# Routing weights applied to the experts' inner values, eight experts summed in one PSUM bank

## The chip, the cores and the metric

The kernel is one program on one core of a Trainium2 chip. A core has five engines with instruction streams of their own, which meet only at semaphores: TensorE (PE, matrix products into PSUM), VectorE (DVE), ScalarE (ACT), GpSimd (POOL) and SyncE (SP, which here issues all DMAs). The metric is the device time of one execution in microseconds (us).

## The reference, cut to what matters

The program is two layers of attention and feed-forward with a layer norm ahead of and behind each. The change lies in the last part, a mixture of eight experts over 2 x 1024 tokens of width 128:

```python
weights = _routing_weights(x, Wr, temperature)      # [tokens, 8]
gate = jnp.einsum('btd,edi->beti', x, Wg)           # inner size I = 128
up = jnp.einsum('btd,edi->beti', x, Wu)
h = jax.nn.silu(gate) * up
e_out = jnp.einsum('beti,eid->betd', h, Wd)
out = jnp.einsum('bte,betd->btd', weights, e_out)
...
x = x + _layernorm(out)                             # of x = _layernorm(...) going in
```

The routing weights come from a sigmoid of `x @ Wr`, a window on its value, two exponentials, and a fallback on the two best experts.

## The kernel before, in words

Tokens are handled in four chunks of 512; two chunks make one batch. In the expert stage the 32 pairs of chunk `c` and expert `e` are numbered n = 8c + e. All data are float32. Every order is written out by hand, in one loop for each engine, and an engine that waits in its list holds up all that stands behind it.

For each n TensorE computes gate and up (`d_up`, L573: two products of 128x512) into one of two pairs of PSUM banks, ScalarE takes silu of the gate (L791), VectorE multiplies by up (`d_hidden`, L1207) into one of two buffers `h_d`, and TensorE multiplies by the expert's down weights (`d_down`, L582: four products of 128x128), one expert behind, so ups and downs alternate. Tokens stand on the partitions of the result, so the routing weight of expert e is one number per partition and block: VectorE multiplies the bank with it (`d_scale`, L1217), and GpSimd adds the eight results of a chunk into `y_a` (L1452 for the first, L1455 for the rest). Then come a layer norm and the addition to `x`: statistics on VectorE (`stats`, L830 and L833), the inverse root on GpSimd (`rstd_of`, L1295 and L1296), the application (`apply`, L840, four parts) and the addition (L850) on VectorE.

Other work is threaded into these loops. The routing weights of the first batch (`route_a`, `route_b`, `route_c`, L1098 to L1138) are computed on VectorE ahead of the loops, those of the second batch within them. The second half of the preceding attention is finished here as well: its head norms (`heads_square`, `heads_b`), the turning of its result (`d_turn_y`), the output product (`d_wo`), its norm c_out of chunks 2 and 3, and the norm d_in, the turning (`d_turn_x`) and the router products of these chunks, without which the experts of chunks 2 and 3 can't begin. GpSimd's inverse roots are done in the order of the table `NORMS`; `apply` waits for the count of its entry.

## Time and profile before

| what | value |
|---|---|
| device time, median of 3 runs | 828.21 us (826.44 to 828.77) |
| span of the profiled execution, first to last instruction | 824.3 us |
| TensorE / VectorE / ScalarE / GpSimd busy in the span | 703.1 / 596.4 / 486.6 / 259.7 us |
| last add of the stage ends (L850) | 821.6 us after the span's start |
| first up product of the stage starts (L573) | 688.1 us |
| mean granted TensorE clock | 0.974 of full speed |

The page gives the profiled execution's time as its span; the runs' median is 3.9 us more, which lies around the span. Times on the trace are counted from the span's start. The expert stage is the last 136 us. Busy time of TensorE counts overlapping, modelled ends, so its share in a stretch says how seldom it waited, not how fast it ran.

### The profile page before, as it was taken

How to read it: one execution, taken by the hardware profiler on the slowest of the kernel's cores; microseconds unless marked ns; L12 is line 12 of the kernel's file. 1: busy time of each engine (PE TensorE's matmuls, PEld its weight loads, DVE VectorE, ACT ScalarE, POOL GpSimd, SP SyncE). 2: the span in 40 equal slices, each digit the busy share in tenths (PEclk: the TensorE clock that was granted, in tenths of full speed). 3: DMA queues.
4: the chain of work that ended last, by engine and by line, in shares of the span. 5: the costliest groups of instructions: out<-in, count | busy, mean ns of one | idle time of the engine just before them, and what ended most of it. 6: DMA issues, size and time to landing. Idle time of an engine off the chain costs nothing.

```text
span 824.3 us, 9749 instructions
## 1 busy us (share of the span) xinstructions
PE 703.1 (85%) x3471; PEld 297.3 (36%) x3512; DVE 596.4 (72%) x1107; ACT 486.6 (59%) x467; POOL 259.7 (32%) x373
## 2 busy tenths in 40 slices
PE   5999899999997689888888988888888884797695
PEld 2576445454544122222222222222222221465353
DVE  4656413226163988988998899999999987669765
ACT  1344424243432688998999999899888883121221
POOL 3601000001026461334226334423330004355254
PEclk9999999999999799999999999999999998799898
DMA  8000200000000000000000000000000000000000
GB/s 285 0 2 2 79 0 0 1 1 0 0 1 0 1 1 1 0 2 1 1 1 1 1 1 0 1 1 1 1 1 1 0 1 1 0 1 14 0 14 26
DMA packets 7152, 9.15 MB, mean 11 GB/s; under 512 B 1216, under 2 KB 5952, under 8 KB 6720
## 3 DMA queue, kind: packets, MB, share of 16 engines
q1 hardware_dynamic: 7104, 8.53, 3.0%
q8 instruction: 28, 0.46, 0.2%
q14 instruction: 20, 0.16, 0.1%
HBM read 7.48 MB, written 1.05 MB: 10 GB/s over the span
## 4 chain that ended last, share of the span: by engine, by line
PE 48%; DVE 35%; ACT 9%; issue 6%; POOL 1%; DMA 1%; SPq 0%; POOLq 0%; DVEq 0%; ACTq 0%
DVE hid L1018 10%; DVE hid L1015 10%; PE ps L453 7%; PE ps L463 7%; ACT probs L740 6%; PE ps L524 6%; PE ps L531 6%; PE ps L573 4%; PE ps L440 3%; PE ps L313 2%; PE ps L582 2%; PE ps L473 2%; PE ps L360 2%; PE ps L391 2%; DVE st L830 1%
## 5 line engine op out<-in xcount | busy, mean ns | idle before, releaser
L756 ACT ACTIVATE w_hh<-hid 128x2048 f32<-128x2048 f32 x128 | 243.8, 1904 | 10.3 <-DVE hid L1018 9.9
L524 PE MATMUL ps<-q_s,k 128*128 128x512 bf16 x496 | 147.5, 387 | 54.4 <-DVE hid L1018 38.2
L1015 DVE TENSOR_TENSOR hid<-ps,probs 128x1024 f32<-128x1024 f32 x128 | 156.2, 1221 | 34.1 <-ACT probs L740 32.7
L740 ACT ACTIVATE probs<-ps,gain 128x1024 f32<-128x1024 f32 x128 | 142.2, 1111 | 46.0 <-PE ps L524 45.4
L1018 DVE SCALAR_TENSOR_TENSOR hid<-ps,probs 128x1024 f32<-128x1024 f32 x128 | 155.5, 1215 | 0.0
L531 PE MATMUL ps<-w_hh,v_h 128*32 128x512 f32 x1024 | 138.1, 611 | 2.1 <-ACT w_hh L756 1.6
L524 PEld LDWEIGHTS ps<-q_s,k 128*128 128x128 bf16 x512 | 37.5, 98 | 150.9 <-DVE hid L1018 90.2
L524 PE MATMUL ps<-q_s,k_s 128*128 128x512 bf16 x231 | 72.3, 386 | 3.4 <-DVE q_s L1029 1.3
L926 DVE SCALAR_TENSOR_TENSOR hid<-ps,s_b,rot 128x512 f32<-128x512 f32 x16 | 11.9, 750 | 87.1 <-ACT rot L713 87.1
L791 ACT ACTIVATE hid<-ps 128x512 f32<-128x512 f32 x32 | 19.0, 598 | 89.0 <-PE ps L573 86.9
L1295 POOL TENSOR_SCALAR rs<-mv 128x4 f32<-128x4 f32 x32 | 7.3, 229 | 172.1 <-DVE mv L833 171.6
L582 PE MATMUL ps<-probs_t,hid 128*128 128x128 f32 x256 | 37.7, 294 | 27.4 <-DVE hid L1207 20.7
L453 PE MATMUL ps<-hid,w_hh 128*128 128x512 f32 x128 | 56.0, 595 | 0.0
L463 PE MATMUL ps<-hid,w_hh 128*128 128x512 f32 x128 | 55.6, 592 | 0.0
L1333 POOL TENSOR_SCALAR u_k<-part 128x128 bf16<-128x128 bf16 x96 | 48.3, 530 | 9.7 <-DVE part L982 9.7
L582 PEld LDWEIGHTS ps<-probs_t,hid 128*128 128x128 f32 x256 | 34.9, 204 | 44.8 <-DVE hid L1207 29.4
L1333 POOL TENSOR_SCALAR u_q<-part 128x128 bf16<-128x128 bf16 x96 | 48.4, 532 | 0.0
L1455 POOL TENSOR_TENSOR y_a<-y_a,hid 128x512 f32<-128x512 f32 x28 | 35.9, 1282 | 25.5 <-DVE hid L1217 24.5
L531 PEld LDWEIGHTS ps<-w_hh,v_h 128*32 128x32 f32 x1024 | 20.6, 108 | 57.8 <-issue 55.2
L524 PEld LDWEIGHTS ps<-q_s,k_s 128*128 128x128 bf16 x256 | 18.2, 98 | 61.0 <-issue 33.6
L1207 DVE TENSOR_TENSOR hid<-ps,hid 128x512 f32<-128x512 f32 x32 | 21.8, 685 | 24.2 <-ACT hid L791 24.0
L1352 POOL TENSOR_SCALAR v_h<-v_c 128x128 f32<-128x128 f32 x16 | 8.9, 554 | 92.4 <-PE ps L531 92.4
(220 smaller groups left out, 958.7 us busy)
## 6 DMA issues: line engine op xcount, KB each, us to landing
w_hh<-in_b_h SPq DMA_DIRECT2D x2, 1024.0 KB, 8.1
x_res<-in_x SPq DMA_DIRECT2D x4, 256.0 KB, 6.4
tab<-in_rope SPq DMA_DIRECT2D x1, 1024.0 KB, 7.7
out<-x_res SPq DMA_DIRECT2D x4, 256.0 KB, 2.3
w<-in_b_w SPq DMA_DIRECT2D x1, 512.0 KB, 5.6
tab<-in_d_wg SPq DMA_DIRECT2D x1, 512.0 KB, 3.5
tab<-in_d_wu SPq DMA_DIRECT2D x1, 512.0 KB, 4.4
probs_t<-in_d_wd SPq DMA_DIRECT2D x1, 512.0 KB, 4.9
```

The source lines that it names most:

```text
L453: last = mm(ps[:, o, :], w_h1[:, k, o * P:(o + 1) * P], hid[:, 0, k, :], start=(k == 0), stop=(k == KT_ - 1))
L463: last = mm(ps[:, o, :], w_h2[:, k, o * P:(o + 1) * P], hid[:, 1, k, :], start=(k == 0), stop=(k == KT_ - 1))
L524: last = mm(ps[:, base + half, :], k_op[:, u, keys], q_s[:, u, half * CHUNK:(half + 1) * CHUNK], start=True, stop=True)
L531: last = mm(ps[VW * g4:VW * g4 + VW, 6, :], v_h[:, u, mt, :], ee[:, mt % 2, g4 * CHUNK:(g4 + 1) * CHUNK], start=(mt == 0), stop=(mt == BT ...
L573: last = mm(ps[:, 2 * (e % 2) + w, :], wt[:, e, :], xt_d[c], start=True, stop=True)
L582: last = mm(ps[:, 4 + e % 2, k * P:(k + 1) * P], h_d[:, e % 2, k * P:(k + 1) * P], w_d[:, e, :], start=True, stop=True)
L740: A(gg[:, mt % 2, :], banks[:, 0:2 * CHUNK], ACT.Tanh, scale=gain[:, u:u + 1]).then_inc(S["g"], 1)
L756: A(ee[:, mt % 2, :], zz[:, mt % 2, :], ACT.Exp).then_inc(S["e"], 1)
L1015: v.tensor_tensor(zz[:, mt % 2, 0:SEQ], banks[:, 2 * CHUNK:4 * CHUNK], gg[:, mt % 2, :], ALU.add).then_inc(S["z1"], 1)
L1018: v.scalar_tensor_tensor(zz[:, mt % 2, SEQ:2 * SEQ], banks[:, 4 * CHUNK:6 * CHUNK], -1.0, gg[:, mt % 2, :], ALU.mult, ALU.subtract).then_i ...
L1333: last = g.tensor_scalar(out_ap, in_ap, 1.0, None, ALU.mult)
L1455: g.tensor_tensor(y_d(c), y_d(c), e_out[:, e % 2], ALU.add).then_inc(S["ad_d"], 1)
```

## The change

The routing weight is applied before the down product instead of after it. There the token runs along the free dimension, so the weight has to be a row of 512 numbers that is the same on all 128 partitions. Once the weights of a batch are computed (`wts`), TensorE turns them (`d_turn_w`), ScalarE copies the 64x128 result to `w_t`, SyncE writes it to a DRAM tensor `w_rows`, waits until it has landed, and reads it back in four transfers, each with four experts' rows of 512 repeated for 128 partitions (1 MB each in SBUF). GpSimd multiplies `h_d` by them in place (32 times), and the down products of a chunk's eight experts add up in one PSUM bank. The multiplication by the weight on VectorE (L1217, 32 times) and the 32 copies and additions on GpSimd (L1452, L1455) are gone; the statistics and the application of the last norm read PSUM.

`h_d` becomes a ring of 12 slots. In each batch the first eleven ups run with no down between them; behind ups 11 to 14 stand three downs each and behind the last one four. The routing of the first batch is laid between the first `d_hidden` calls, that of the second batch behind those of n = 21, 23 and 24, and the attention's rest stands at other n. `NORMS` has a new order: c_out 2, c_out 3, d_in 2, d_in 3, d_out 0.

```diff
-         ("d_in", 1), ("c_out", 2), ("d_out", 0), ("d_in", 2), ("c_out", 3), ("d_in", 3), ("d_out", 1),
+         ("d_in", 1), ("c_out", 2), ("c_out", 3), ("d_in", 2), ("d_in", 3), ("d_out", 0), ("d_out", 1),
...
+ND = CHUNKS * EXPERTS
+SLOTS = 12
+
+
+def downs_after(n):
+
+    b, i = divmod(n, ND // BATCH)
+    if i == ND // BATCH - 1:
+        return n + 1
+    return b * (ND // BATCH) + (min(3 * (i - SLOTS + 2), i - 1) if i >= SLOTS - 1 else 0)
...
-        wts = sb("wts", [P, BATCH, BT, EXPERTS])
-        sg_d, h_d = (flat_hid[:, 2 * CHUNK * i:2 * CHUNK * (i + 1)].rearrange("p (a b) -> p a b", a=2)
-                     for i in range(2))
-        e_out = flat_hid[:, 4 * CHUNK:6 * CHUNK].rearrange("p (a b c) -> p a b c", a=2, b=CT)
+        wts = sb("wts", [P, BATCH, EXPERTS, BT])
+        w_t = sb("w_t", [P // 2, P])
+        w_rows = nc.dram_tensor("w_rows", (BATCH, EXPERTS, SEQ), F32, kind="Internal").ap()
+        sg_d = u_q[:].rearrange("p a b c -> p (a b c)").bitcast(F32).rearrange("p (a b) -> p a b", a=2)
+        h_d = flat_hid.rearrange("p (a b) -> p a b", a=SLOTS)
+        flat_hh = w_hh[:].rearrange("p a b c -> p (a b c)")
+        part_f = [w[:].rearrange("p a b c -> p (a b c)").bitcast(F32) for w in part[:2]]
+        half_e = EXPERTS // 2
+        w_b = [[flat_hh[:, i * half_e * CHUNK:(i + 1) * half_e * CHUNK].rearrange("p (a b) -> p a b", a=half_e)
+                for i in range(2)], [w.rearrange("p (a b) -> p a b", a=half_e) for w in part_f]]
...
+            for b in range(BATCH):
+                sp.wait_ge(S["wt_d"], b + 1)
+                sp.dma_start(w_rows[b].rearrange("e (t k) -> (e t) k", t=BT), w_t[:]).then_inc(S["w_out"], 16)
+                sp.wait_ge(S["w_out"], 16 * (b + 1))
+                for half in range(2):
+                    if b:
+                        sp.wait_ge(S["hw_d"], EXPERTS * (half + 1))
+                    for g in range(2):
+                        src = w_rows[b][g * half_e:(g + 1) * half_e, half * CHUNK:(half + 1) * CHUNK]
+                        sp.dma_start(w_b[half][g], src.unsqueeze(0).to_broadcast([P, half_e, CHUNK])
+                                     ).then_inc(S[f"w_in{half}{g}"], 16)
...
             def d_down(c, e):
                 n = EXPERTS * c + e
-                pe.wait_ge(S["h_d"], n + 1)
-                if n >= 2:
-                    pe.wait_ge(S["sc_d"], n - 1)
+                pe.wait_ge(S["hw_d"], n + 1)
+                if c >= 2 and e == 0:
+                    pe.wait_ge(S["xfin"], c - 1)
                 for k in range(CT):
-                    last = mm(ps[:, 4 + e % 2, k * P:(k + 1) * P], h_d[:, e % 2, k * P:(k + 1) * P],
-                              w_d[:, e, :], start=True, stop=True)
+                    last = mm(ps[:, 4 + c % 2, k * P:(k + 1) * P], h_d[:, n % SLOTS, k * P:(k + 1) * P],
+                              w_d[:, e, :], start=(e == 0 and k == 0), stop=(e == EXPERTS - 1),
+                              skip_group_check=True)
                 last.then_inc(S["eo_d"], 1)
...
+            def d_turn_w(b):
+                pe.wait_ge(S["wts_d"], b + 1)
+                if b:
+                    pe.wait_ge(S["xt_d"], 2)
+                nc.tensor.transpose(ps[0:P // 2, BANK_TURN, 0:P], wts[:, b].rearrange("p e t -> p (e t)"),
+                                    ident[:]).then_inc(S["wtp_d"], 1)
...
-            for c in range(CHUNKS):
-                for e in range(EXPERTS):
-                    d_up(c, e)
...
+            downs = 0
+            for n in range(ND):
+                c, e = divmod(n, EXPERTS)
+                d_up(c, e)
+                if n in (8, 25):
+                    d_turn_w(n // 16)
+                if n in (10, 11):
+                    d_turn_y(n - 8)
+                if n in (11, 12):
+                    d_wo(n - 9)
+                for m in range(downs, downs_after(n)):
+                    d_down(*divmod(m, EXPERTS))
+                downs = max(downs, downs_after(n))
+                if n in (14, 16):
+                    d_turn_x(n // 2 - 5)
+                if n == 18:
+                    d_route(2)
                     d_route(3)
...
+            def d_wt(b):
+                act.wait_ge(S["wtp_d"], b + 1)
+                if b:
+                    act.wait_ge(S["w_out"], 16)
+                A(w_t[:], ps[0:P // 2, BANK_TURN, 0:P], ACT.Copy).then_inc(S["wt_d"], 1)
+
             d_gate(0)
             d_exps(0)
-            for c in range(CHUNKS):
-                for e in range(EXPERTS):
-                    n = EXPERTS * c + e
...
+            for n in range(ND):
+                e = n % EXPERTS
+                act.wait_ge(S["gu_d"], n + 1)
+                if n >= 2:
+                    act.wait_ge(S["h_d"], n - 1)
+                A(sg_d[:, e % 2, :], ps[:, 2 * (e % 2), :], ACT.Silu).then_inc(S["sg_d"], 1)
+                if n in (8, 25):
+                    d_wt(n // 16)
+                if n in (10, 11):
+                    d_yt(n - 8)
+                if n in (14, 16):
+                    d_xt(n // 2 - 5)
+                if n == 20:
                     d_gate(1)
+                if n == 22:
+                    d_exps(1)
...
-            def d_hidden(c, e):
-                n = EXPERTS * c + e
+            def d_hidden(n):
+                e = n % EXPERTS
                 dve.wait_ge(S["sg_d"], n + 1)
-                if n >= 2:
-                    dve.wait_ge(S["eo_d"], n - 1)
-                v.tensor_tensor(h_d[:, e % 2, :], ps[:, 2 * (e % 2) + 1, :], sg_d[:, e % 2, :],
+                if n >= SLOTS:
+                    dve.wait_ge(S["eo_d"], n - SLOTS + 1)
+                v.tensor_tensor(h_d[:, n % SLOTS, :], ps[:, 2 * (e % 2) + 1, :], sg_d[:, e % 2, :],
                                 ALU.mult).then_inc(S["h_d"], 1)

-            def d_scale(c, e):
-
-                n = EXPERTS * c + e
...
+            def sum_d(c):
+                return ps[:, 4 + c % 2, :].rearrange("p (a b) -> p a b", a=CT)
...
+            def d_out_add(c):
+                apply("d_out", c, sum_d(c), y_d(c))
+                v.tensor_tensor(x_of(c), x_of(c), y_d(c), ALU.add).then_inc(S["xfin"], 1)
...
             route_a(0)
-            route_b(0)
-            route_c(0)
-            for c in range(CHUNKS):
...
+            for n in range(ND):
+                d_hidden(n)
+                if n == 0:
+                    route_b(0)
+                if n == 2:
+                    route_c(0)
+                if n == 6:
+                    heads_square(1)
+                    for i in range(3):
+                        rsqrt_newton(rstd[:, 0:W2], W2, "ms_o" if i == 2 else None)
+                if n == 11:
+                    wo_bias(2)
+                    stats("c_out", 2, y[:])
+                if n == 12:
+                    add_out("c_out", 2, y[:])
+                    wo_bias(3)
+                    stats("c_out", 3, y[:])
+                    stats("d_in", 2, x_of(2))
+                if n == 13:
+                    d_in_apply(2)
+                    add_out("c_out", 3, y[:])
+                    stats("d_in", 3, x_of(3))
+                if n == 14:
+                    d_in_apply(3)
+                if n in (15, 17, 30):
+                    d_out_stats({15: 0, 17: 1, 30: 2}[n])
+                if n in (16, 18, 31):
+                    d_out_add({16: 0, 18: 1, 31: 2}[n])
+                if n == 19:
                     dve.wait_ge(S["rt_d"], 2)
                     for half in range(2):
                         logits(half, ps[:, 6, half * CT * EXPERTS:(half + 1) * CT * EXPERTS]).then_inc(S["z_d"], 1)
+                if n == 21:
+                    route_a(1)
+                if n == 23:
+                    route_b(1)
+                if n == 24:
+                    route_c(1)
             d_out_stats(CHUNKS - 1)
-            add_out("d_out", CHUNKS - 1, y_d(CHUNKS - 1), "xfin")
+            d_out_add(CHUNKS - 1)
...
-            for c in range(CHUNKS):
-                for e in range(EXPERTS):
-                    n = EXPERTS * c + e
...
+            heads_b(1)
+            for n in range(ND):
+                c, e = divmod(n, EXPERTS)
+                b, half = divmod(c, 2)
+                pool.wait_ge(S["h_d"], n + 1)
+                if e % half_e == 0:
+                    pool.wait_ge(S[f"w_in{half}{e // half_e}"], 16 * (b + 1))
+                g.tensor_tensor(h_d[:, n % SLOTS, :], h_d[:, n % SLOTS, :], w_b[half][e // half_e][:, e % half_e, :],
+                                ALU.mult).then_inc(S["hw_d"], 1)
+                if n in (2, 3):
+                    rstd_of("c_out", n)
+                if n in (5, 7):
+                    rstd_of("d_in", n // 2)
+                if n in (13, 15, 29):
+                    rstd_of("d_out", {13: 0, 15: 1, 29: 2}[n])
             rstd_of("d_out", CHUNKS - 1)
```

TensorE around n = 6 to 9, before. L573 is an up product (two rows each), L582 a down product, L313 a turning, L597 the output product.

```order
L573 MATMUL ps<-xt,tab 128x512 x2
L582 MATMUL ps<-probs_t,hid 128x128 x4
L313 MATMUL ps<-ident,xn_c 128x128 x4
L573 MATMUL ps<-xt,tab 128x512 x2
L582 MATMUL ps<-probs_t,hid 128x128 x4
L597 MATMUL ps<-w_os,w 128x128 x4
L582 MATMUL ps<-probs_t,hid 128x128 x4
L573 MATMUL ps<-xt_c,tab 128x512 x2
```

TensorE from n = 9 to 13 now. L602 is the up product, L611 the down product, L342 and L620 turnings, L636 the output product.

```order
L602 MATMUL ps<-xt_c,tab 128x512 x4
L342 MATMUL ps<-ident,xn_c 128x128 x4
L602 MATMUL ps<-xt_c,tab 128x512 x2
L342 MATMUL ps<-ident,y_c 128x128 x4
L636 MATMUL ps<-w_os,w 128x128 x4
L611 MATMUL ps<-probs_t,hid 128x128 x12
L602 MATMUL ps<-xt_c,tab 128x512 x2
L636 MATMUL ps<-w_os,w 128x128 x4
L611 MATMUL ps<-probs_t,hid 128x128 x12
L602 MATMUL ps<-xt_c,tab 128x512 x2
L611 MATMUL ps<-probs_t,hid 128x128 x12
```

Before, one down follows each up; now the first three downs (12 products of L611) stand behind the twelfth up and both turnings, and the thirteenth up stands behind these three.

GpSimd, chunks 0 and 1, before: L1452 and L1455 are the sums, L1295 with L1296 an inverse root.

```order
L1455 TENSOR_TENSOR y_a<-y_a,hid 128x512 x5
L1295 TENSOR_SCALAR rs<-mv 128x4
L1296 TENSOR_TENSOR rs<-rs,half_down 128x4
L1452 TENSOR_SCALAR y_a<-hid 128x512
L1295 TENSOR_SCALAR rs<-mv 128x4
L1296 TENSOR_TENSOR rs<-rs,half_down 128x4
L1455 TENSOR_TENSOR y_a<-y_a,hid 128x512
```

GpSimd now: L1490 is the multiplication by the routing weights, L1333 with L1334 an inverse root.

```order
L1490 TENSOR_TENSOR hid<-hid,w_hh 128x512 x3
L1333 TENSOR_SCALAR rs<-mv 128x4
L1334 TENSOR_TENSOR rs<-rs,half_down 128x4
L1490 TENSOR_TENSOR hid<-hid,w_hh 128x512
L1333 TENSOR_SCALAR rs<-mv 128x4
L1334 TENSOR_TENSOR rs<-rs,half_down 128x4
L1490 TENSOR_TENSOR hid<-hid,w_hh 128x512 x2
```

The inverse roots now stand between multiplications for which the down products wait: c_out 2 behind n = 2, c_out 3 behind n = 3, d_in 2 behind n = 5 (and, not shown, d_in 3 behind n = 7, d_out 0 behind n = 13, d_out 1 behind n = 15).

## Rows read from the trace of the kernel before

**Rows 1.** Busy us by stretch and engine (instructions), clock, DMA share, GB/s.
```profile
777.00:814.00 37.00, 35.36 (x154) 22.23 (x155) 24.90 (x46) 7.19 (x12) 20.82 (x18) 0.94 0.05 15
```

**Rows 2.** Chain that ended last, expert stage: start, us, engine, tile, line, count.
```profile
807.93 1.72 PE ps L573 x4
809.65 0.89 PE ps L582 x8
...
729.62 0.44 PE ps L313 x4
...
817.00 0.88 DVE st L830 x4
817.91 0.39 DVE mv L833 x4
...
820.90 0.69 DVE x_res L850
```

**Rows 3.** Waits of TensorE, 704 to 825: total, times, longest.
```profile
PE ps L582 <- DVE hid L1207: 20.7, 7, 13.1
PE ps L582 <- DVE hid L1217: 6.4, 1, 6.4
```

**Rows 4.** Timeline of TensorE: start, us, instruction, idle before it and releaser.
```profile
704.92 2.07 PE L582 MATMUL ps<-probs_t,hid 128*128 128x128 f32 x8 [13.10 <-DVE hid L1207]
...
706.79 3.20 PE L573 MATMUL ps<-xt,tab 128*128 128x512 f32 x4
...
719.30 1.16 PE L582 MATMUL ps<-probs_t,hid 128*128 128x128 f32 x8 [1.48 <-DVE hid L1207]
...
743.79 2.07 PE L582 MATMUL ps<-probs_t,hid 128*128 128x128 f32 x8 [3.29 <-DVE hid L1207]
```

**Rows 5.** Timeline of VectorE and ScalarE: routing, head norms, table load.
```profile
693.05 1.08 DVE L1109 TENSOR_TENSOR w_a<-w_a 128x64 f32<-128x64 f32 x1
...
700.27 0.69 DVE L1117 TENSOR_REDUCE w_a<-raw 128x64 f32<-128x512 f32 x1
...
703.92 0.22 DVE L1138 TENSOR_TENSOR wts<-w_a,rs 128x64 f32<-128x64 f32 x1
...
714.47 0.68 DVE L1084 TENSOR_REDUCE ms_o<-probs_t 128x32 f32<-128x512 f32 x1
...
718.41 0.23 DVE L818 SCALAR_TENSOR_TENSOR rstd<-nt,rstd 128x64 f32<-128x64 f32 x1
...
763.68 1.28 ACT L770 ACT_TABLE_LOAD   x1
```

**Rows 6.** Groups by line, 687.5 to 825: count, busy us, mean ns, idle before.
```profile
L1455 POOL TENSOR_TENSOR y_a<-y_a,hid 128x512 f32<-128x512 f32 x28 | 35.9, 1282 | 25.5 <-DVE hid L1217 24.5
...
L1207 DVE TENSOR_TENSOR hid<-ps,hid 128x512 f32<-128x512 f32 x32 | 21.8, 685 | 24.2 <-ACT hid L791 24.0
...
L791 ACT ACTIVATE hid<-ps 128x512 f32<-128x512 f32 x32 | 19.0, 598 | 89.0 <-PE ps L573 86.9 <-DVE hid L1207 2.0
...
L1296 POOL TENSOR_TENSOR rs<-rs,half_down 128x4 f32<-128x4 f32 x8 | 8.4, 1052 | 0.7
```

**Rows 7.** Timeline of VectorE: the four-part apply (L840), three cases.
```profile
752.64 2.06 DVE L840 TENSOR_SCALAR y_a<-y_a,mv,rs 128x128 f32<-128x128 f32 x4
...
780.35 3.01 DVE L840 TENSOR_SCALAR y_a<-y_a,mv,rs 128x128 f32<-128x128 f32 x4
...
819.75 1.11 DVE L840 TENSOR_SCALAR y_a<-y_a,mv,rs 128x128 f32<-128x128 f32 x4 [1.47 <-POOL rs L1296]
```

**Rows 8.** DMA issues: tile, queue, count, KB each, us to landing.
```profile
w_hh<-in_b_h SPq DMA_DIRECT2D x2, 1024.0 KB, 8.1
...
out<-x_res SPq DMA_DIRECT2D x4, 256.0 KB, 2.3
...
w<-in_b_w SPq DMA_DIRECT2D x1, 256.0 KB, 9.7
```

**Rows 9.** Busy time by stretch, while three weight loads run.
```profile
92.00:94.00 2.00, 2.00 (x6) 0.89 (x5) 0.00 (x0) 0.96 (x1) 0.27 (x1) 1.00 1.04 420
```

More of the change, by code:

```diff
@@ L229, in sandwich @@
             ro to_a ms_o yc ytp yt wo wo_read xn_d tp_d xt_d rt_d z_d tanh_d dist_d ex_d
-            gu_d sg_d h_d eo_d sc_d ad_d xfin stored""".split()
+            gu_d sg_d h_d hw_d eo_d wts_d wtp_d wt_d w_out w_in00 w_in01 w_in10 w_in11 xfin stored""".split()
         S = {n: sem("e_" + n) for n in names}
@@ L604, in d_turn_x @@
                     pe.wait_ge(S["xt_d"], c - 2)
-                turn_chunk(xn).then_inc(S["tp_d"], 1)
+                turn_chunk(xn_2[c % 2]).then_inc(S["tp_d"], 1)
             def d_route(c):
@@ L1119, in route_c @@
             def route_c(b):
-                w = wts[:, b]
+                w = wts[:, b].rearrange("p e t -> p t e")
                 wide = [P, BT, EXPERTS]
@@ L1137, in route_c @@
                 me.step(v.reciprocal(rs1[:, 2], rs1[:, 0]))
-                me.step(v.tensor_tensor(w, rt[:, 3], rs1[:, 2].unsqueeze(2).to_broadcast(wide), ALU.mult))
+                v.tensor_tensor(w, rt[:, 3], rs1[:, 2].unsqueeze(2).to_broadcast(wide), ALU.mult).then_inc(S["wts_d"], 1)
             turn_out(("k", 0))
@@ new lines, in d_out_stats, with d_in_apply @@
+                dve.wait_ge(S["eo_d"], EXPERTS * (c + 1))
+                stats("d_out", c, sum_d(c))
+            def d_out_add(c):
+                apply("d_out", c, sum_d(c), y_d(c))
+                v.tensor_tensor(x_of(c), x_of(c), y_d(c), ALU.add).then_inc(S["xfin"], 1)
+            def d_in_apply(c):
+                if c == 3:
+                    dve.wait_ge(S["ytp"], 1)
+                else:
+                    dve.wait_ge(S["turned"], turns_done(("x", 1)))
+                apply("d_in", c, x_of(c), xn_2[c % 2][:], "xn_d")
@@ L1442, in _ @@
             heads_a(1)
-            for c in range(CHUNKS):
-                for e in range(EXPERTS):
-                    n = EXPERTS * c + e
-                    pool.wait_ge(S["sc_d"], n + 1)
-                    if e == 0:
-                        if c >= 2:
-                            pool.wait_ge(S["xfin"], c - 1)
-                        g.tensor_scalar(y_d(c), e_out[:, 0], 1.0, None, ALU.mult).then_inc(S["ad_d"], 1)
-                    else:
-                        pool.wait_ge(S["ad_d"], n)
-                        g.tensor_tensor(y_d(c), y_d(c), e_out[:, e % 2], ALU.add).then_inc(S["ad_d"], 1)
-                    at = (c, e)
-                    if at == (0, 2):
-                        heads_b(1)
-                    if at == (0, 7):
-                        rstd_of("c_out", 2)
-                    if at == (1, 0):
-                        rstd_of("d_out", 0)
-                    if at == (1, 1):
-                        rstd_of("d_in", 2)
-                        rstd_of("c_out", 3)
-                    if at == (1, 3):
-                        rstd_of("d_in", 3)
-                    if c >= 2 and e == 0:
-                        rstd_of("d_out", c - 1)
+            heads_b(1)
[13 more added lines that the diff above has]
+                    rstd_of("d_out", {13: 0, 15: 1, 29: 2}[n])
             rstd_of("d_out", CHUNKS - 1)
```

78 lines of the change are left out of this document (3 added, 75 removed).

## The prediction

> **What bounds the kernel now.** I read the stretches first. Late in the expert stage (777 to 814 us) TensorE is busy 35.4 of 37 us [rows 1], but over the whole stage it isn't. The chain of waits gives what it needs there: an up product 1.72 us, a down product 0.89, a turning 0.44 [rows 2]. The stage has 32 ups (55.0), 32 downs (28.5), four turnings (1.8), and two output and two router products of eight passes each like a down (3.6): 88.8 us. From the first up at 688.1 to the end of the last down at about 814.5 are 126.4 us. The difference of 37.6 us has two parts. TensorE waited for VectorE's products and scalings 20.7 + 6.4 us, 13.1 of it once, while VectorE computed the first routing weights [rows 3], and 1.4 us elsewhere. The other 9 us are a lower clock: behind waits of 13.1 and 3.3 us a down took 2.07 us instead of 1.16, behind 1.5 us it did not [rows 4]. So the stage is bound by lists of four engines that wait for each other, and by TensorE's work in its second half. VectorE's 0.69 us scaling and GpSimd's 1.28 us sum per expert [rows 6] mostly lie beside TensorE. Behind the last down come 7.1 us to the last addition.
>
> **How I work it out.** I laid the new lists of all engines end to end: each instruction starts when its engine is free and what it waits for has ended, with durations of the rows. The old lists laid out so end at 821.2 us; the trace has 821.6. I add that 0.4.
>
> Durations: up 1.72, down 0.89 [rows 2]; silu 0.60, `d_hidden` 0.64 to 0.69 [rows 6]; statistics 1.25 and the addition 0.69 [rows 2]; an inverse root 1.4 from the end of the statistics to the apply (817.91 + 0.39 to 819.75) [rows 2, 7]. GpSimd's multiplication is not in the trace; the nearest row is its sum of two SBUF operands of the same 512 at 1.28 us, and I take that. Its bounds are 1.05 (the cheapest GpSimd row, L1296) and 1.4 (two VectorE products of 0.69 one behind the other) [rows 6].
>
> The apply has three prices: 1.11 us with GpSimd idle, 2.06 and 3.01 with its sums under way [rows 7]. By my layout GpSimd waits during most applies of the new lists, so they get 1.11, but d_in 3 gets 3.0 and d_out 2 gets 2.06. The Trainium skill, "SBUF — State Buffer", section "Who interferes with whom", says that VectorE's two-port modes and its instructions with two SBUF inputs share one port pair with GpSimd, a lock held for the whole instruction. By that rule 1.11 would hold wherever GpSimd waits, as the rows say; if instead 2.06 held for five of these applies, the sum would be 4.3 us higher.
>
> DMA: `w_rows` is written in 2.3 us, as the 256 KB stores are [rows 8]. While three weight loads run, the queues move 420 GB/s [rows 9], which is 2.5 us for 1 MB. The first of the four broadcasts lands 2.3 + 2.5 = 4.8 us after its issue, the others 2.5 us apart. The trace has no transfer that reads one place 128 times. Bounds: 2.3 us for the first load, if its bytes cost nothing beyond a small transfer, and upward 8.1 us for each 1 MB one behind the other (the landing of `w_hh`), or even 38.8 us, if a megabyte moved at the worst row, 256 KB in 9.7 us [rows 8]. I take the rate of rows 9, since size and partitions are those of its loads.
>
> **The change part by part, by TensorE's waits.**
> - Start. `d_hidden(0)` stands behind `route_a` and the scalar engine's exponentials, `d_hidden(1)` and (2) behind `route_b`, which takes 7.2 us beside GpSimd's `heads_a`. Up 2 waits 3.2 us (to 694.8), up 3 4.4 us (to 702.6). The routing weights, ready at 704.1 before [rows 5], are ready at 706.4 but no longer hold TensorE 13.1 us. The head norms (714.47 to 718.64, 4.2 us [rows 5]) behind n = 6 hold up 9 for 2.5 us.
> - First weights. `d_turn_w(0)` stands behind up 8 and ends at 715.1; copy 0.3, store 2.3 and first load 4.8 lead to 723.0. Up 11, both turnings and output product 2 cover this: down 0 starts at 724.6 and the three downs wait 0.6 together.
> - n = 12. The root of c_out 3 stands on GpSimd ahead of multiplication 4. It needs statistics that VectorE makes behind `d_hidden(12)`, apply, addition, bias. Up 12 ends 729.5; 0.6 + 0.7, then 1.1 + 0.7 + 0.7 + 1.2 give 734.6; root 1.3 and multiplication 1.3 give 737.2. TensorE ended down 3 at 731.3: a wait of 5.9.
> - n = 13. Up 13 ends 742.7, its product 744.0; apply d_in 2, apply and addition c_out 3 and statistics d_in 3 (1.1 + 1.1 + 0.7 + 1.2) lead to 748.2, root and multiplication 8 to 750.8. TensorE ended down 7 at 744.5: a wait of 6.4.
> - n = 15. Root d_out 0 stands ahead of multiplication 14 and needs statistics behind `d_hidden(15)`, 762.8: multiplication 14 ends 765.4, TensorE waits 3.4. Down 15 ends at 769.0.
> - Ups 16 to 25 run at 1.72 each, with two waits of 0.8 together at most, then the second routing: `d_hidden(23)` waits for two table loads (1.28 each [rows 5]) and the exponentials, `route_b` takes 3.5 (five wide operations of 0.69 [rows 5]), `route_c` 3.1. Up 25 waits 1.6, the turning of weights, placed behind it, waits 5.5 more, until 795.7.
> - Second weights. Copy, store, load and first multiplication take 8.8 us behind 796.2; only ups 26 and 27 cover it. Down 16 waits 3.7 and starts at 805.0.
> - From there 16 downs and four ups are 21.1 us, a restart 1.9: the last down ends at 828.1. GpSimd, 16 multiplications and a root, keeps just ahead.
> - Behind it: 4.9 us (statistics 1.2, 0.5 late since d_out 2 is just being added, root 1.4, apply 1.1, addition 0.7) instead of 7.1, since scaling and sum are gone.
>
> The clock: seven waits above are over 3 us (3.2, 4.4, 5.9, 6.4, 3.4, 5.5, 3.7). The rows give 0.9 us for the down alone behind 3.3 us, and 2.07 + 3.20 against 1.16 + 1.72, or 2.4, behind 13.1 [rows 2, 4]. I take 1.9 each, 13.4 in all, against 9.1 now.
>
> The sum for TensorE: work 89.3, waits 37.3, clock 13.4 = 140.0 us, from 688.1 to 828.1. Against now: work +0.5, waits +8.8 (37.3 against 28.5), clock +4.3, tail -2.2: 11.4, with rounding 11.5. The span would be 835.8 us instead of 824.3. The runs lie 3.9 us above the span, so 828.2 + 11.6 = 839.8, **840 us**, 1.4% slower. What is removed, 22 us of VectorE and 42 of GpSimd, was hidden except in the tail; GpSimd gets 41 us of multiplications back.
>
> **The rivals.**
> 1. The broadcast loads are slow. For: all 128 partitions read the same 8 KB, which no row shows. Against: every row of large transfers is near 400 GB/s. At 8.1 us each, the last group of weights lands 20 us later in either batch (32.4 against 12.3); laid out, the span is 850.4, the time 854. At 38.8 us each it is 1080 (time 1084). The Trainium skill, "SBUF — State Buffer", section "A bandwidth-pool intuition that's wrong (but worth ruling out)", gives 22.5 GB/s for one port of the HBM crossbar; if all reads fell on one, 1 MB would take 47 us by that page, an estimate, beyond even my worst row.
> 2. Waits of 3 to 6 us leave the clock up. For: behind 1.5 us it stayed. Against: 3.3 us was enough once. All seven restarts off give a span of 828.4, time 832; with a multiplication of 1.04 and the fastest loads besides, 824.2, time 828: no change.
> 3. Faster: GpSimd's roots don't hold the multiplications, because VectorE reaches the statistics of c_out 3, d_in 3 and d_out 0 early, so that downs 4, 8 and 14 find their operand. That takes off 15.7 us of waits and three restarts of 1.9: 840 - 21.4 = 818 us. It decides from where these three waits fall below 2.5 us in all. Against: up 12 and up 13 stand behind the downs that wait, so VectorE can't be early; this is in the lists, not in durations.
>
> **How the numbers follow.** The forecast, 833 to 847, has 0.62. Rival 1 has 0.20, rival 2 0.12 (half of it at 826 to 831), rival 3 0.06. A measurement tells 0.3%, 2.5 us, from no change. Faster by more: 0.06. Within: 0.06, all from rival 2. Slower: 0.88. The range leaves out rival 3 and the far part of rival 1: 829 to 862.
>
> **What would show it.** TensorE should wait once each at the down products 4, 8 and 14 for GpSimd, about 6, 6 and 3 us, and for VectorE at the second turning of weights, 5 to 6. The four broadcasts should land 4.8 us after issue and 2.5 apart, the multiplication should take 1.3, the clock should fall behind each wait over 3 us, and the last down should end 4 to 5 us ahead of the last addition. I am wrong if the multiplications take clearly over 1.3 (with 1.6 the span is 840.4), if a broadcast takes over 6 us, or if TensorE doesn't wait at downs 4 and 8.

## The result, and the profile after

The changed kernel takes 843.29 us (median of 4 runs, 840.16 to 843.8), the kernel before beside it 827.43 (826.44 to 828.77): a ratio of 1.0184, 95% interval 1.0168 to 1.0200. It is slower, by 1.8%. The forecast was 840, within 829 to 862. The profiled execution has a span of 838.4 us, where 835.8 was worked out.

By stretch, in the columns of [rows 1]:

```profile
688.00:704.00 16.00, 8.82 (x15) 3.30 (x16) 14.64 (x29) 3.37 (x6) 9.51 (x8) 0.73 0.00 1
704.00:736.00 32.00, 24.25 (x95) 13.49 (x94) 18.54 (x62) 7.22 (x13) 9.88 (x11) 0.93 0.41 132
736.00:777.00 41.00, 30.13 (x135) 22.19 (x136) 11.97 (x42) 4.58 (x8) 18.18 (x18) 0.79 0.00 1
777.00:814.00 37.00, 25.90 (x81) 13.72 (x81) 16.77 (x50) 9.16 (x17) 9.36 (x9) 0.91 0.33 110
```

From 777 to 814 TensorE was busy 35.4 us before [rows 1] and is busy 25.9 now: the stretch that TensorE filled has become one of waits. Between 736 and 777 the mean clock is 0.79. No other engine is near full there (VectorE 12 of 41 us, GpSimd 18): nothing is overloaded, the lists wait for each other. The waits of TensorE, 686 to 840, against [rows 3]:

```profile
PE ps L611 <- POOL hid L1490: 19.9, 4, 6.4
PE ps L602 <- DVE hid L1254: 11.6, 5, 4.2
PE ps L620 <- DVE wts L1185: 5.4, 1, 5.4
```

The timeline of TensorE at these waits (L602 up, L611 down, L620 turning of weights; L1490 is GpSimd's multiplication, L1254 the inner value), against [rows 4]:

```profile
694.63 3.05 PE L602 MATMUL ps<-xt,tab 128*128 128x512 f32 x4 [2.98 <-DVE hid L1254]
701.88 10.71 PE L602 MATMUL ps<-xt,tab 128*128 128x512 f32 x20 [4.20 <-DVE hid L1254]
...
736.98 3.78 PE L611 MATMUL ps<-probs_t,hid 128*128 128x128 f32 x16 [6.09 <-POOL hid L1490]
740.55 3.20 PE L602 MATMUL ps<-xt_c,tab 128*128 128x512 f32 x4
743.58 1.95 PE L611 MATMUL ps<-probs_t,hid 128*128 128x128 f32 x16
751.92 2.08 PE L611 MATMUL ps<-probs_t,hid 128*128 128x128 f32 x8 [6.39 <-POOL hid L1490]
...
767.32 3.56 PE L611 MATMUL ps<-probs_t,hid 128*128 128x128 f32 x16 [3.50 <-POOL hid L1490]
...
798.06 0.42 PE L620 MATMUL ps<-ident,wts 128*64 128x128 f32 x1 [5.35 <-DVE wts L1185]
...
807.21 4.70 PE L611 MATMUL ps<-probs_t,hid 128*128 128x128 f32 x24 [3.87 <-POOL hid L1490]
```

Behind the wait of 6.09 us two downs take 3.57 us from start to start and the up 3.03, against 1.78 and 1.72 at full clock. From 743.58 on two downs show 1.95, so the clock is back. On GpSimd the waits of 6.09, 6.39 and 3.50 us end in the same way (the first two are shown; the one of 3.87 ends with a DMA landing):

```profile
734.34 0.23 POOL L1333 TENSOR_SCALAR rs<-mv 128x4 f32<-128x4 f32 x1 [5.47 <-DVE mv L880]
734.66 1.03 POOL L1334 TENSOR_TENSOR rs<-rs,half_down 128x4 f32<-128x4 f32 x1
735.66 2.49 POOL L1490 TENSOR_TENSOR hid<-hid,w_hh 128x512 f32<-128x512 f32 x2
...
749.29 0.23 POOL L1333 TENSOR_SCALAR rs<-mv 128x4 f32<-128x4 f32 x1 [7.37 <-DVE mv L880]
749.61 1.03 POOL L1334 TENSOR_TENSOR rs<-rs,half_down 128x4 f32<-128x4 f32 x1
750.61 7.39 POOL L1490 TENSOR_TENSOR hid<-hid,part 128x512 f32<-128x512 f32 x6
```

GpSimd idles 5.5 and 7.4 us for statistics (`mv`), makes the inverse root, and only then multiplies the value that TensorE wants; six multiplications had piled up behind the second. The DMA issues, in the columns of [rows 8]:

```profile
w_hh<-w_rows SPq DMA_DIRECT2D x4, 1024.0 KB, 7.4
part<-w_rows SPq DMA_DIRECT2D x4, 1024.0 KB, 12.7
```

These are medians of four, two in each batch. All four loads of a batch are issued together, so later ones count the time of those ahead. The first lands within 5.5 us of its issue at 716.92 (GpSimd's first multiplication starts at 722.43), the slowest load 13.7 us after its own issue. The transfers of the first batch end at about 731.6.

### The profile page after: what moved, and what is told of

Same layout as the page of the kernel before. It is cut to its first block, busy times and chain, and to the rows that moved or that the text cites. A ratio compares the mean times of both kernels' runs of the same rounds, so it can differ in the third digit from the quotient of the medians.

```text
span 838.4 us, 9688 instructions
## 1 busy us (share of the span) xinstructions
PE 716.5 (85%) x3514; PEld 302.1 (36%) x3514; DVE 569.4 (68%) x1075; ACT 486.7 (58%) x469; POOL 256.9 (31%) x373
## 3 DMA queue, kind: packets, MB, share of 16 engines
HBM read 15.87 MB, written 1.11 MB: 20 GB/s over the span
## 4 chain that ended last, share of the span: by engine, by line
PE 49%; DVE 32%; ACT 9%; issue 5%; DMA 2%; POOL 2%; SPq 0%; POOLq 0%; ACTq 0%; DVEq 0%
DVE hid L1065 10%; DVE hid L1062 10%; PE ps L482 7%; PE ps L492 7%; PE ps L553 6%; ACT probs L780 6%; PE ps L560 6%; PE ps L602 4%; PE ps L611 3%; PE ps L469 3%; PE ps L342 2%; PE ps L502 2%; PE ps L389 2%; PE ps L420 2%; DMA w_hh<-w_rows 1%
## 5 line engine op out<-in xcount | busy, mean ns | idle before, releaser
L553 PE MATMUL ps<-q_s,k 128*128 128x512 bf16 x512 | 151.0, 387 | 51.4 <-DVE hid L1065 36.0
L553 PE MATMUL ps<-q_s,k_s 128*128 128x512 bf16 x256 | 77.8, 386 | 1.1 <-DVE q_s L1076 1.1
L836 ACT ACTIVATE u_q<-ps 128x512 f32<-128x512 f32 x32 | 18.9, 597 | 101.1 <-PE ps L602 101.0
L1254 DVE TENSOR_TENSOR hid<-ps,u_q 128x512 f32<-128x512 f32 x32 | 21.9, 689 | 71.3 <-ACT u_q L836 71.1
L1333 POOL TENSOR_SCALAR rs<-mv 128x4 f32<-128x4 f32 x32 | 7.3, 229 | 193.7 <-DVE mv L880 193.3
L611 PE MATMUL ps<-probs_t,hid 128*128 128x128 f32 x256 | 37.7, 309 | 20.0 <-POOL hid L1490 19.9
L611 PEld LDWEIGHTS ps<-probs_t,hid 128*128 128x128 f32 x256 | 36.1, 221 | 26.1 <-POOL hid L1490 22.0
L1387 POOL TENSOR_SCALAR gain<-gains 128x1 f32<-128x1 f32 x16 | 3.8, 236 | 104.7 <-ACT probs L780 104.7
```

The source lines that it names most:

```text
L553: last = mm(ps[:, base + half, :], k_op[:, u, keys], q_s[:, u, half * CHUNK:(half + 1) * CHUNK], start=True, stop=True)
L611: last = mm(ps[:, 4 + c % 2, k * P:(k + 1) * P], h_d[:, n % SLOTS, k * P:(k + 1) * P], w_d[:, e, :], start=(e == 0 and k == 0), stop=(e == ...
```

## The experiments

Each ran three rounds beside the kernel before; times are medians, spans those of the profiled executions. All but the run on the kernel before are edits of the changed kernel.

**Roots later in GpSimd's list.**

```diff
-                if n in (2, 3):
-                    rstd_of("c_out", n)
-                if n in (5, 7):
-                    rstd_of("d_in", n // 2)
...
+                if n in (2, 7):
+                    rstd_of("c_out", {2: 2, 7: 3}[n])
+                if n in (7, 11):
+                    rstd_of("d_in", {7: 2, 11: 3}[n])
+                if n == 15:
+                    rstd_of("d_out", 0)
+                    rstd_of("d_out", 1)
```

> The changed kernel with five of GpSimd's inverse roots moved back behind multiplications that don't need them: c_out 3 and d_in 2 behind n = 7 (were 3 and 5), d_in 3 behind n = 11 (was 7), d_out 0 behind n = 15 (was 13). No instruction is added or removed. Theory A (the order of GpSimd's list holds down products 4, 8 and 14 by 6.1, 6.4 and 3.5 us, and each such wait brings 1.6 to 3.1 us of lower clock): laying the lists out gives a wait of 2 us at down 8 and none at 4 and 14, a span near 817 instead of 838.4, so about 822 us, 2.5% under the changed kernel and below the kernel before (827.4). Rival B (VectorE's work at n = 12 and 13 is what ends last; the roots only mark it): the waits move to the applies and stay, span above 833, time above 836.

Measured 827.95 us (10 runs), ratio to before 1.0007, 0.9989 to 1.0024; span 826.6. The waits at downs 4 and 14 are gone (one of 1.1 us is left at down 15), and 15.3 of the 15.9 us that the change had cost came back: with the roots out of the way the loss is gone. But 822 was expected, from a span of 817. Of these 9.6 us of span 2.9 lie ahead of down 0, which starts at 726.84 here and at 723.99 in the changed kernel, although the lists are the same up to there. The lower clock was held longer in this execution; first the changed kernel's row, then this one's:

```profile
687.95 3.70 PE L602 MATMUL ps<-xt,tab 128*128 128x512 f32 x8 [0.53 <-DVE qkv_a L1078]
```

```profile
688.59 6.41 PE L602 MATMUL ps<-xt,tab 128*128 128x512 f32 x8 [0.53 <-DVE qkv_a L1078]
```

The larger part lies behind it. VectorE's applies, and GpSimd's row of multiplications beside each:

```profile
732.68 4.04 DVE L887 TENSOR_SCALAR y<-y,mv,rs 128x128 f32<-128x128 f32 x4
...
742.36 4.89 DVE L887 TENSOR_SCALAR xn<-x_res,mv,rs 128x128 f32<-128x128 f32 x4 [1.12 <-POOL rs L1334]
747.17 1.10 DVE L887 TENSOR_SCALAR y<-y,mv,rs 128x128 f32<-128x128 f32 x4
```

```profile
730.46 6.18 POOL L1490 TENSOR_TENSOR hid<-hid,w_hh 128x512 f32<-128x512 f32 x5
...
742.22 4.94 POOL L1490 TENSOR_TENSOR hid<-hid,part 128x512 f32<-128x512 f32 x4
```

A set of four parts takes 4.04 and 4.89 us while GpSimd multiplies, and 1.10 once it has stopped (747.17). A third took 3.92. That is some 9.5 us more on VectorE than at 1.1 each. The wait at down 8 was 4.6 us instead of the 2 expected. That the slow applies are the whole of the rest isn't shown: no run on these lists has them fast.

**Filler products in TensorE's waits.** Of products whose results aren't used, 6 stand before down 4, 6 before down 8, 3 before down 14, 5 before the second turning of weights and 3 before down 16.

```diff
+            def keep_busy(at, pe):
...
+                for i in range(count):
+                    mm(ps[:, bank, :], ident[:], xt_c[:], start=True, stop=True)
```

> The changed kernel with products that nobody reads put into TensorE's five long waits (6, 6, 3, 5 and 3 products of 128x512 float32 at 0.86 us, ahead of down products 4, 8, 14, of the second turning of weights and of down product 16). It leaves nothing out. Theory A (about 10 us of the changed kernel's time is TensorE at half the clock behind these waits: 3.1, 2.5, 1.6, 1.6, 1.9 by its trace): the products behind them run at 0.89 and 1.72, the span falls by 7 to 10 us to about 830, since some of it comes back as longer waits for the loads. Rival B (the clock behind a wait costs nothing, as GpSimd's 1.25 us per expert sets the pace there): the span stays within 2 us of 838.4, or grows by fillers that run past the end of a wait.

Measured 836.39 us, ratio 1.0105 (1.0084 to 1.0126), 6.9 below the changed kernel. The span is 835.4, only 3.0 below, where 7 to 10 were expected. But this execution, too, came late to the part that the filler touches: down 0 starts at 728.11 instead of 723.99. From there to the end of the last down it is 99.7 us against 106.8, 7.1 less. Behind the wait at down 4 two downs and the up now run at full clock:

```profile
740.55 2.38 PE L611 MATMUL ps<-probs_t,hid 128*128 128x128 f32 x16 [0.94 <-POOL hid L1501]
742.77 1.88 PE L602 MATMUL ps<-xt_c,tab 128*128 128x512 f32 x4
...
804.42 4.57 PE L611 MATMUL ps<-probs_t,hid 128*128 128x128 f32 x24 [2.73 <-POOL hid L1501]
```

Against 3.78 and 3.20 us above (the 2.38 contain a wait for multiplication 5). At down 16 the three products of filler were too few: a wait of 2.7 us was left, and the three downs behind it still take 4.42 us from start to start, against 4.54 above and 2.67 at full clock. So the clock was lost through the waits. Where about 1 us of wait was left, at four of the five places, it stayed up, and what came back is the lower end of what theory A named.

**One set of weights.** The second batch takes the first batch's weights: its turning, store and loads are left out.

```diff
-            for b in range(BATCH):
+            for b in range(1):
...
-                if n in (8, 25):
-                    d_turn_w(n // 16)
+                if n == 8:
+                    d_turn_w(0)
```

> The changed kernel without the second trip of the weights: no second turning, copy, store or loads, and GpSimd multiplies the second batch by the first batch's weights (so the output of the second batch is weighted wrongly; VectorE still computes its weights). Theory A (the second trip costs TensorE 5.4 us ahead of the turning and 3.9 ahead of down product 16, and two restarts of the clock, less what VectorE's routing then holds): the span falls by 9 to 10 us to about 829. Rival B (VectorE's routing at n = 23 and 24 holds TensorE just as long at the ups behind it): under 5 us. Rival C (GpSimd's 16 multiplications from n = 16 on bound the end): they start earlier too, so it agrees with A; it would be seen by waits at each down product.

Measured 836.89 us, ratio 1.0121 (1.0102 to 1.0141): 6.4 less, between the two expectations. The waits of 5.4 and 3.9 us are gone, but VectorE's routing then holds an up, which was covered before:

```profile
796.42 3.78 PE L602 MATMUL ps<-qkv_a,tab 128*128 128x512 f32 x4 [3.32 <-DVE hid L1254]
```

TensorE's waits for VectorE's inner values rose from 11.6 to 16.8 us: more than half of the 9.2 us removed came back, by the way that rival B named. The span fell by 4.0 us, the median by 6.4.

**The kernel before, with its first two inner values ahead of the routing.**

```diff
             route_a(0)
+            d_hidden(0, 0)
             route_b(0)
+            d_hidden(0, 1)
             route_c(0)
```

> The kernel before with one part of the change alone, routing in pieces: the products of n = 0 and 1 on VectorE stand behind route_a and route_b instead of behind all three. Theory A: TensorE's wait of 13.1 us becomes waits of about 3, 3 and 2 us, downs 0 and 1 are done before the weights are ready; laid out, the span falls by 5.8 us to 818.5, time about 821.6. Rival B (the scalings need the weights anyway, and TensorE waits at down 2 for what it saved): the span within 2 us of 824.3.

Measured 821.48 us, ratio 0.9933 (0.9919 to 0.9948), as expected to 0.2 us; the span is 819.9, for 818.5. The one wait of 13.1 us in [rows 3] has become two, of 1.6 and 4.2 us (about 3, 3 and 2 were expected). From 686 us on:

```profile
PE ps L582 <- DVE hid L1207: 12.9, 8, 4.2
```

So the routing in pieces is worth 6 us by itself, and the changed kernel, which has it too, lies 22 us above this one.

**Applies with three operands** (those of c_out and d_in for chunks 2 and 3), on the roots-later kernel, and as a control on the changed kernel.

```diff
                 for k in range(CT):
+                    if kind in ("c_out", "d_in") and c >= 2:
+                        last = v.scalar_tensor_tensor(dst[:, k, :], src[:, k, :], mv[:, i, k, 0:1],
+                                                      rs[:, i, k:k + 1].to_broadcast([P, P]), ALU.subtract, ALU.mult)
+                        continue
                     last = v.tensor_scalar(dst[:, k, :], src[:, k, :], mv[:, i, k, 0:1], rs[:, i, k:k + 1],
                                            ALU.subtract, ALU.mult)
```

> The kernel with the roots later (the run before), with one thing more: the c_out and d_in applies of chunks 2 and 3 are written as scalar_tensor_tensor, (x - mean) * rstd with rstd broadcast along the row as the third operand, in place of tensor_scalar. Same reads, same writes, same place in VectorE's list, one operand more. Theory A: the tensor_scalar from SBUF is held until GpSimd's row of multiplications has ended (4.04, 4.89 and 3.92 us in the run before, each ending within 0.4 us of the end of GpSimd's row), and the form with three operands isn't: then each set of four takes 1.3 to 1.5 us, the waits for the two chunks' experts shrink, and the time falls by 7 to 11 us, to 817 to 821 us. Rival B: any VectorE work with SBUF operands slows beside GpSimd's multiplications (both move the same bytes): then the four take 3 us or more and the time stays at 826 to 830.

> Control: the changed kernel with only the form of these applies changed as in the run beside it; the roots stay where the change has them. GpSimd is idle while these applies run (1.11 us for four, all four sets), so both theories expect nothing to win: four would take 1.3 to 1.4 us in place of 1.11, and the time stays within 1.5 us of the changed kernel's 843.3 (842 to 845). Should it come out 3 us or more faster, the gain of the run beside it would not be the port's but the form's.

Measured 828.08 us (10 runs, ratio 1.0016, 0.9998 to 1.0035) and 843.02 (1.0207, 1.0176 to 1.0237). The control came as expected; the first did not: the sets took 4.26, 5.10 and 4.09 us.

```profile
732.20 0.69 DVE L1258 TENSOR_TENSOR hid<-ps,u_q 128x512 f32<-128x512 f32 x1 [3.02 <-ACT u_q L836]
...
742.69 5.10 DVE L888 SCALAR_TENSOR_TENSOR xn<-x_res,mv,rs 128x128 f32<-128x128 f32 x4 [1.11 <-POOL rs L1338]
747.71 1.13 DVE L888 SCALAR_TENSOR_TENSOR y<-y,mv,rs 128x128 f32<-128x128 f32 x4
```

My choice of form was poor: it reads two tensors from SBUF. The Trainium skill, "SBUF — State Buffer", section "Who interferes with whom", has that case beside the two-port modes as the two that take the ports shared with GpSimd, and these runs agree: part by part, one beside the row takes 1.30 us in the old form and 1.35 in the new, about one multiplication of 1.25, against 0.33 and 0.34 alone. (In the sets of 4.04 and 3.92 us one part of the four ran free.) Rival B got the time right, and is wrong only in its "any": an inner value (one operand in PSUM, one in SBUF) takes 0.69 us beside the row too (732.20), and an apply from PSUM isn't slowed. In the changed kernel the last but one apply has a multiplication beside it:

```profile
828.10 1.36 DVE L887 TENSOR_SCALAR y_a<-ps,mv,rs 128x128 f32<-128x128 f32 x4
828.26 1.27 POOL L1490 TENSOR_TENSOR hid<-hid,part 128x512 f32<-128x512 f32 x1 [0.59 <-DVE hid L1254]
...
833.55 1.37 DVE L887 TENSOR_SCALAR y_a<-ps,mv,rs 128x128 f32<-128x128 f32 x4 [1.47 <-POOL rs L1334]
```

1.36 us beside GpSimd, 1.37 without. The next two kernels have lists laid out before this was known, on theory A's 1.4 us for every apply.

**All lists rewritten**, with either form of the apply.

```diff
+PE_TURN_W = {6: 0, 22: 1}
+PE_TURN_X = {14: 2, 16: 3}
+ROOTS = {1: ['c2'], 5: ['c3', 'di2'], 9: ['di3'], 14: ['do0'], 17: ['do1'], 29: ['do2']}
+DVE_STEPS = {1: ['rb0a', 'rb0b'], 2: ['rb0c', 'rb0d'], 4: ['rc0a', 'rc0b'], 5: ['hsqa'], ...}
...
+                for name in DVE_STEPS.get(n, ()):
+                    step[name]()
```

> The changed kernel (broadcast weights, one bank per sum, ring of 12) with the order of every list written anew: first routing cut into six pieces between the hidden values of experts 1 to 4, first weights turned behind up 6 (not 8), the second routing's steps behind hidden values 16 to 20 and its weights turned behind up 22 (not 25), no root in GpSimd's list ahead of a multiplication that a down waits for (roots behind multiplications 1, 5, 9, 14, 17, 29), downs spread between the ups from up 10 on, applies with three operands. Laid end to end with the measured durations (up 1.72, down 0.89, multiplication 1.25, apply 1.4) TensorE waits 3.1 us at up 2 and under 1 us anywhere else, the last down ends near 786, and the span is 793: time 794 to 802. Theory A (the loss of the change is its waits, their clock, and a list that leaves VectorE no room): within that. Rival B (the broadcast's DMAs and 32 multiplications on GpSimd slow the others once they run side by side): 808 or more.

> The same lists as the run beside it, with the applies in the old form (tensor_scalar). Under theory A (port held by GpSimd's rows) at least two of the four sets of applies fall beside a row of multiplications and take 3 to 5 us: 3 to 10 us more than the run beside it, 800 to 808. Under B of the first of these runs: within 1.5 us of the run beside it.

Measured 810.53 us (ratio 0.9803, 0.9780 to 0.9825) and 810.33 (0.9801, 0.9785 to 0.9817): faster than every kernel so far, 8.5 to 16.5 us above theory A's 794 to 802, in rival B's range (808 or more), and no difference between the forms. In the first of the two:

```profile
720.56 5.18 DVE L896 SCALAR_TENSOR_TENSOR y<-y,mv,rs 128x128 f32<-128x128 f32 x4 [0.89 <-POOL rs L1346]
...
732.41 5.12 DVE L896 SCALAR_TENSOR_TENSOR xn<-x_res,mv,rs 128x128 f32<-128x128 f32 x4 [0.96 <-POOL rs L1346]
...
742.75 5.10 DVE L896 SCALAR_TENSOR_TENSOR xn_c<-x_res,mv,rs 128x128 f32<-128x128 f32 x4 [1.53 <-POOL rs L1346]
```

Each of these follows on a root, and so does GpSimd's row of multiplications: a root ends, both engines start, and they collide all three times. Three sets at 5.1 instead of 1.4 are 11 us on VectorE, and TensorE waited 2.5, 2.1 and 2.8 us behind them. So rival B was right that the multiplications slow VectorE once they run side by side; of the broadcasts' DMAs this doesn't show it.

**The apply in two instructions over 512 elements**: on the roots-later kernel, on these lists, and on lists laid out again with 2.7 us for an apply.

```diff
+                if kind in ("c_out", "d_in") and c >= 2:
+                    me.step(v.tensor_tensor(dst, src, mv[:, i, :, 0:1].to_broadcast([P, CT, P]), ALU.subtract))
+                    last = v.tensor_tensor(dst, dst, rs[:, i, :].unsqueeze(2).to_broadcast([P, CT, P]), ALU.mult)
```

> The kernel with the roots later, with the c_out and d_in applies of chunks 2 and 3 in two instructions over all 512 elements (subtract the mean, then multiply by rstd, both broadcast along the row) in place of four instructions over 128. In both earlier forms each of the four took about 1.3 us beside GpSimd's row of multiplications, which is the time of one multiplication (1.25), and 0.28 us without. Theory C (an instruction of VectorE whose operands all lie in SBUF waits for the GpSimd instruction that is running, once per instruction, whatever its size and form): two instructions take 1.4 us without and 2.0 to 2.7 beside the row; three sets lie beside a row, each gets 1.4 to 2.5 shorter, and the time is 821 to 825 us. Rival D (VectorE gets a share of the bytes, or is held until GpSimd's row ends): they take 4 us or more, and the time stays at 827 to 830.

> The rewritten lists of the runs before (810.5 and 810.3 us) with the applies in two instructions. There three sets took 5.1 us each beside GpSimd's rows, and TensorE waited 2.5, 2.1 and 2.8 us behind them and then ran 7 to 9 us below full clock. Theory C: the sets take 2.0 to 2.7, these three waits fall under 1 us, the span is 797 to 802 and the time 799 to 804. Rival D: 809 to 812.

> The lists laid out once more, now with 2.7 us for an apply beside a row of multiplications: first weights turned behind up 5, first products of the output projection behind ups 8 and 10, second turned behind 14 and 18, roots behind multiplications 0, 5, 8, 15 and 31. Laid end to end the waits are 3.1 us at up 2 and at most 2.1 at the first weights, none behind up 10. Theory C: 797 to 803 us, within 3 us of the run beside it; rival D: 806 or more.

Measured 829.41 us (9 runs, ratio 1.0027, 1.0015 to 1.0040), 809.02 (0.9789, 0.9770 to 0.9807) and **801.74** (0.9701, 0.9685 to 0.9717). On the roots-later kernel the two engines now look like this:

```profile
740.96 1.68 DVE L887 TENSOR_TENSOR xn<-x_res,mv 128x512 f32<-128x512 f32 x1 [1.11 <-POOL rs L1338]
742.67 1.65 DVE L888 TENSOR_TENSOR xn<-xn,rs 128x512 f32<-128x512 f32 x1
744.24 1.75 DVE L887 TENSOR_TENSOR y<-y,mv 128x512 f32<-128x512 f32 x1
746.02 1.63 DVE L888 TENSOR_TENSOR y<-y,rs 128x512 f32<-128x512 f32 x1
747.69 0.69 DVE L901 TENSOR_TENSOR x_res<-x_res,y 128x512 f32<-128x512 f32 x1
```

```profile
740.83 6.28 POOL L1494 TENSOR_TENSOR hid<-hid,part 128x512 f32<-128x512 f32 x4
```

Neither C nor D, though the time is the one that D gave: an instruction of 0.69 us takes 1.65 beside the row, so a set is 3.3 to 3.4 rather than 2.0 to 2.7, and the multiplications slow too, to 1.57 each (6.28 / 4) from 1.24. The row thus lasts longer and catches the next set, at 744.24, which ran free before. What one set gained the next one lost, and the time did not fall. I could have read this price beforehand. In the changed kernel a wide operation of the routing runs once beside GpSimd's head norms and once alone:

```profile
696.07 1.59 POOL L1439 TENSOR_TENSOR y_a<-y_a 128x512 f32<-128x512 f32 x1
696.46 1.75 DVE L1161 TENSOR_TENSOR raw<-w_a 128x512 f32<-128x512 f32 x1
...
791.32 0.68 DVE L1161 TENSOR_TENSOR raw<-w_a 128x512 f32<-128x512 f32 x1
```

On the first rewritten lists (809.02) the outcome was rival D's as well: TensorE still waited up to 3.2 us for an apply. The lists laid out again fell into theory C's 797 to 803, but not for C's reason: their applies cost 3.4 beside a row, not the 2.7 laid out, and they were to be within 3 us of the run beside them. That the time came out is in part luck. The last run has only waits of 1.1 us and less behind 716 us, and a full clock from 704 to 768:

```profile
704.00:736.00 32.00, 27.85 (x125) 16.60 (x125) 27.30 (x69) 7.89 (x14) 19.20 (x17) 1.00 0.42 133
736.00:768.00 32.00, 30.23 (x138) 18.82 (x139) 22.21 (x66) 10.64 (x19) 14.25 (x14) 1.00 0.18 51
```

It does all of the change's work, in some 41 us less than the changed kernel and 25.0 less than the kernel before beside it (826.75). Its gain over the first rewritten lists with the same applies, 7.3 us, is the order of the lists alone.

## Why the prediction was right

The likeliest case came true, and mostly by its own steps; three of its terms were right or close by luck, and are named below. From the first up to the end of the last down 140.0 us were worked out and 142.8 measured (687.95 to 830.7).

- **Waits.** The ten in the view add up to 36.8 us. The first three downs, in one row at 723.99, wait 0.6 more between them (3.23 us from start to start instead of 2.67), as forecast; that makes 37.4 against 37.3. At downs 4, 8 and 14: 6.1, 6.4, 3.5 (5.9, 6.4, 3.4 forecast); ups 2, 3, 9: 3.0, 4.2, 2.6 (3.2, 4.4, 2.5); up 25 and the turning 1.6 and 5.4 (1.6, 5.5); down 16 3.9 (3.7). That the roots cause the first three was shown by moving them.
- **Clock.** 13.4 taken. From start to start the seven restarts cost 1.2 and 1.9 (ups 2 and 3), 3.1, 2.5, 1.6, 1.5 and 1.9: 13.7 together. The sum was right, the flat 1.9 each was not, so that the sum fits is luck in part. The single costs aren't fixed either: in the run with one set of weights the waits of 6.09, 6.39 and 3.50 us cost 1.7, 1.8 and 2.9 where they cost 3.1, 2.5 and 1.6 here. The filler gave back 6.9 of the 10.6 that its five places cost; at down 16 it gave back nearly nothing, and behind the waits at 4 and 14 two downs then took 2.22 us, not 1.78, as the second waits for its multiplication.
- **The rest** of the 2.8 us is 2.4: my durations run from start to start, so each wait leaves out the end of the product ahead of it, which no next one overlaps. A single up shows 1.88 us and counts 1.72: 0.16 us at ten waits is 1.6. The last four downs took 0.5 more than 3.56. These terms were missing; 0.3 stays open.
- **DMA.** First landing 5.5 us behind the issue instead of 4.8, but the store (1.8, not 2.3) and what lies ahead were shorter, and the first multiplication starts at 722.4 (723.0 forecast, though 715.1 + 0.3 + 2.3 + 4.8 is 722.5). That it fits is two errors that cancel. The multiplications take 1.25 us each, not 1.28. The rate of [rows 9] was too high: in six stretches of 2 us from 718 to 730 the broadcasts moved 221 to 407 GB/s, 319 on the mean, with the DMA engines busy, against 420, and all four had landed some 14.7 us behind the first issue instead of 12.3. Whether the common source takes this isn't shown. No wait of TensorE came of the later loads, and 14.7 is far from rival 1's 32.4 us. The argument against that rival, that every row of large transfers is near 400 GB/s, was weaker than it reads: only [rows 9] is, and the 8.1 us of [rows 8] for 1 MB aren't.
- **Applies.** The one forecast at 3.0 us (d_in 3) took 1.11, since GpSimd's six multiplications ended half a microsecond ahead of it, at 758.0; the one forecast at 2.06 reads PSUM and took 1.36. Neither lies on the path, so both misses were free. The view behind them, that the price depends on what GpSimd does, was in [rows 7] and carried no term of the sum. Nor are there three prices: part by part the trace of before shows 0.33 us alone and 1.30 beside a sum, so 2.06 is a set with one slow part and 3.01 one with two. A set wholly beside GpSimd, which costs 4.9, wasn't among the rows. In the experiments this price became the largest term.
- **Tail.** 4.9 us as forecast (830.7 to 835.6), by luck: the last statistics weren't 0.5 us late, and the last apply, which reads PSUM, took 1.37 instead of 1.1, with 0.2 more on statistics and root.
- **Above the span.** 3.9 us taken. In every run the time is only 1.8 us above its own span; the rest of the 3.9 was that the profiled execution of before was quicker than the median. Here the median lies 4.9 above the profiled span, as this execution was the quickest of the four; that and the 2.6 us of span are, but for rounding, the 3.5 us missed (839.8).

Rival 2, a clock that stays up, is ruled out by the durations behind the waits, and the filler run shows what they cost. Rival 3 failed as argued: VectorE could not be early. The 818 us that it named, with the roots' waits gone, are 10 below what moving the roots gave (828), and they aren't the floor either.

What the steps implied and I had not said: the loss is in the order of four lists. With the weights' way through memory and all 32 multiplications kept, another order gives 801.7 us (with the applies in two instructions, which gave about 1 us on the lists before). What the kernel before would gain from lists laid out with the same care wasn't tried, beyond the 6 us for its first routing; so what the change itself is worth stays open.

## What to carry to other kernels

Moving work off VectorE and GpSimd bought nothing here while the lists of several engines waited for each other: lay all of them end to end first, and look for a small step (a root of 1.3 us) that stands ahead of something the next engine needs. A wait of TensorE costs its length and then the clock behind it, 1.2 to 3.1 us behind waits of 3.0 to 6.4 us here. Where a result of GpSimd sets off a step of VectorE whose operands lie in SBUF, and GpSimd goes on with work of its own in SBUF, the two collided at once in these kernels; give VectorE's step a source in PSUM, or lay it out at its slow price.

## What the runs showed of the hardware that I had not expected

- An apply from SBUF beside GpSimd's multiplications takes 3.9 to 5.2 us for four parts instead of 1.1: 1.30 to 1.35 us, about one multiplication (1.25), for each part of 0.33 that lies beside the row, in tensor_scalar and scalar_tensor_tensor alike. In instructions of 512 elements it is 1.65 instead of 0.69, and GpSimd slows from 1.24 to 1.57. With its source in PSUM it stays at 1.36. A form with a single SBUF operand that doesn't slow beside GpSimd was not looked for.
- Four loads of 1 MB, each written to 128 partitions from the same 8 KB: the first lands in 5.5 us, all four in some 14.7, at 319 GB/s on the mean. Loads of 1 MB of separate rows took 8.1 us each to land [rows 8].
- A wait near 2.6 us decides nothing by its length alone. Behind the 2.56 us ahead of up 9 the changed kernel's two ups take 3.70 us, at a granted clock of 1.00 of full speed; behind the same wait of 2.55 in the roots-later kernel they take 5.21, starting at 0.50.
